# All six rank steps of the 2-of-4 choice on the vector engine, none on GpSimd

## The chip, the core and the metric

One core of a Trainium2 chip runs the whole program as one launch. Its engines run their own instruction streams and meet only at semaphores: TensorE (PE in the profile), VectorE (DVE), ScalarE (ACT), GpSimd (POOL) and SyncE (SP), which issues the DMAs. The metric is the device time of one execution in microseconds, as the median of several runs.

## What is computed

The input is 2 sequences of 2048 tokens of width 256. Four layers follow one another, each with a residual and a layer normalisation: an attention over channels, an MLP with 4-bit weights, a state-space layer, and a gated MLP that keeps 2 of every 4 hidden values. The change touches the last one alone:

```python
def _sparsify_2to4(h):
    g = h.reshape(B, S, I // 4, 4)
    a = jnp.abs(g)
    _, idx = jax.lax.top_k(a, 2)
    pos = jnp.arange(4)
    mask = (pos == idx[..., 0:1]) | (pos == idx[..., 1:2])
    return (g * mask.astype(g.dtype)).reshape(B, S, I)
h = jax.nn.silu(jnp.einsum('bsh,hi->bsi', x, w_gate)) * jnp.einsum('bsh,hi->bsi', x, w_up)
h_sparse = _sparsify_2to4(h)
return jnp.einsum('bsi,ih->bsh', h_sparse, w_down)
```

The hidden width I is 1024. The result goes through one more residual and layer normalisation.

## The kernel before

The first three layers take the time up to about 1067 us of the profiled span and are not touched. The last stage works on 8 groups of 512 tokens. The hidden values of a group are two units of 4 x 128 channels, so there are 16 units, m = 0 to 15; unit m belongs to group m // 2. Within a unit the index r = 0 to 3 is the place of a channel in its foursome, so the four values that compete lie in four tiles `dh[:, mb, r]` of 128 x 512 at the same address of each. Matmuls run at fp32 accuracy as three passes over a high and a low part (`exact3`, lines 44 to 46), so every operand of a matmul needs its low part, which is the value less its rounded copy.

The engines do for each unit, in a static order:

- TensorE, per r: the gate and the up projection (`gate_and_up`, 12 matmuls of 512 columns), then the down projection of the unit two before (`down1`, 12 matmuls of 256 columns), which needs `dhh` and `dhl`. In the second unit of a group, at r = 1, eight transposes of the next group's input stand between (L1616). The first projection of a group waits for the group's low parts `xt_l`, which VectorE makes in `x3_lo` at the end of the unit before. The projection r + 2 waits for `gated1` of r (semaphore `d_mul`).
- ScalarE, per r: silu of the gate (L916), the absolute value of `dh` (L951) and, in r = 2 and 3, the rounded copies `dhh` of the unit before (`kept_hi`, a copy recorded at L670), two in each r. It also makes the high parts of the next input and keeps the residual.
- VectorE, per r: one part of the choice for the unit before (`sparsify`), then `gated1` of this unit (L1279). Part 0 compares value 0 with values 1 to 3, part 1 compares 1 with 2 and 3 and 2 with 3 (L1297: the six `beats` tiles, bf16 zeros and ones). Part 2 forms the ranks (`add_ranks`) and keeps r = 0 and 1 (`keep`, L1313), part 3 keeps r = 2 and 3. In the first unit of a group the output of the group two before is finished between these: `add_x3` (L1337) ahead of part 0, `out_stats` (L1036) ahead of part 1, `normalise` (L1346) ahead of part 3. The last unit of a group ends with `x3_lo` (L1023) for the next one.
- GpSimd, per unit: `ranks`, two steps each for ranks 2 and 3 (L641, L642, L644, L646), then the four subtractions that give `dhl` (L653). The first unit of a group is preceded by `inv_std` (L520, L522) for the output being finished.

A rank is a sum of the comparisons that concern one value. VectorE sums ranks 0 and 1 in three instructions (L1302 of 1024 columns, L1304 and L1305 of 512), GpSimd sums ranks 2 and 3 in four of 512 columns, at the same time, from the same `beats`. The keeps of r = 0 and 1 wait for `d_add` (VectorE), those of r = 2 and 3 for `d_padd` (GpSimd). GpSimd's order puts the ranks of a unit ahead of its subtractions. Groups 2 to 6 run in a loop over the groups; after the last projections the tail on VectorE is `add_x3`, the whole choice for unit 15, then the output of groups 6 and 7, where group 7 waits for the store of group 6 (one output buffer `rows_out`).

Of the kernel before, what the change touches and what calls it, by code (L numbers as in the profile page):

```python
# [5 lines left out]
ALU = mybir.AluOpType  # L6
# [27 lines left out]
RANK = 4  # L34
MB = MLP1 // RANK // P
DT_STEPS = 11
FIX = 5
RES = 4
W1_PIECE = 3 * KT * MLP1 // GROUPS
# [9 lines left out]
def build(nc, x_in, xt_in, codes, scales, w_in, conv_w, conv_b, dt_bias, a_log, d_skip, norm_w, w_out, w_mlp1, out):  # L49
    ctx = ExitStack()  # L50
    with ctx:
# [3 lines left out]
        def sem(name):  # L55
            return ctx.enter_context(nc.semaphore(name))
# [161 lines left out]
        def ds(name, shape, dt=F32):  # L218
            return sb(name, shape, dt, phase_d)
# [6 lines left out]
        beats = ds("beats", [P, 6, TOK], BF16)  # L226
        rank = ds("rank", [P, RANK, TOK], BF16)
# [112 lines left out]
        d_mul = sem("mlp1_gated_ready")  # L340
        d_abs = sem("mlp1_abs_ready")
        d_cmp = sem("pairs_compared")
        d_add = sem("ranks_dve")
        d_padd = sem("ranks_pool")
        d_sel = sem("kept_ready")
        d_hi = sem("kept_hi_ready")
        d_lo = sem("kept_lo_ready")
# [16 lines left out]
        PAIRS = [(0, 0, 3), (1, 3, 2), (2, 5, 1)]  # L364
# [129 lines left out]
        def _(pool):  # L494
# [53 lines left out]
            def halo_terms(n, b):  # L548
# [5 lines left out]
                pool.tensor_tensor(hpart[:, 1, :, 0:1], tail[:, b, :, 2:3], weight[2], ALU.mult).then_inc(c_fix, 1)  # L554
                pool.wait_ge(c_fix, FIX * n + 2)
                pool.tensor_tensor(hfix[:, b, :, 0:2], hfix[:, b, :, 0:2], hpart[:, 0, :, 0:2], ALU.add).then_inc(c_fix, 1)
                pool.wait_ge(c_fix, FIX * n + 4)
                pool.tensor_tensor(hfix[:, b, :, 0:1], hfix[:, b, :, 0:1], hpart[:, 1, :, 0:1], ALU.add).then_inc(c_fix, 1)
# [7 lines left out]
            def masked_decay(n, t):  # L566

                if t == 0:
                    pool.wait_ge(c_dtc, DT_STEPS * (n + 1))
                    pool.wait_ge(c_seg, NT * n)  # L570
# [65 lines left out]

            pool.wait_ge(c_x3, NT * GROUPS)

            def ranks(m):
                pool.wait_ge(d_cmp, len(PAIRS) * (m + 1))  # L640
                pool.tensor_tensor(rank[:, 2], beats[:, 5], beats[:, 1], ALU.subtract).then_inc(d_padd, 1)  # L641
                pool.tensor_tensor(rank[:, 3], beats[:, 2], beats[:, 4], ALU.add).then_inc(d_padd, 1)  # L642
                pool.wait_ge(d_padd, 4 * m + 1)
                pool.tensor_tensor(rank[:, 2], rank[:, 2], beats[:, 3], ALU.subtract).then_inc(d_padd, 1)  # L644
                pool.wait_ge(d_padd, 4 * m + 2)
                pool.tensor_tensor(rank[:, 3], rank[:, 3], beats[:, 5], ALU.add).then_inc(d_padd, 1)  # L646

            def unit(m, mb):

                ranks(m)  # L650
                for r in range(RANK):
                    pool.wait_ge(d_hi, RANK * m + r + 1)
                    pool.tensor_tensor(dhl[:, mb, r], dab[:, mb, r], dhh[:, mb, r].bitcast(F32),  # L653
                                       ALU.subtract).then_inc(d_lo, 1)

            for m in range(3):
                unit(m, m % MB)
            with pool.Fori(2, GROUPS) as g:
                inv_std(g - 2, mv, ve, rstd, d_ln, d_lnr)
                unit(MB * g - 1, 1)  # L660
                unit(MB * g, 0)
# [6 lines left out]
        def _(act):  # L668
            def copy(dst, src):
                return act.activation(dst, src, ACT.Copy)  # L670
# [96 lines left out]
            def xbc_in(n, b, j, place=None, in_xc=False):  # L767

                src = place if place is not None else XBC_LANE[j]
                act.wait_ge(c_xbc, XB * n + j + 1)  # L770
                if place is None:
                    act.wait_ge(c_silu, XB * n + max(j - 1, 0))
                act.wait_ge(c_fix, FIX * (n + 1))
                copy(tail[:, b, j], src[:, TOK - TAPS + 1:])
                act.activation(xc[:, b, j] if in_xc else acc[:, j % 2], src[:], ACT.Identity, bias=cb[:, j:j + 1],
                               scale=cw[:, j, TAPS - 1:TAPS]).then_inc(c_xin, 1)
# [16 lines left out]
            def dt_exp_ln(n, b, mid=True):  # L793
                act.wait_ge(c_dtc, DT_STEPS * n + 2)
                act.activation(de[:], dax[:], ACT.Exp).then_inc(c_dta, 1)
                if mid:
                    xbc_in(n, b, 0)
                act.wait_ge(c_dtc, DT_STEPS * n + 3)
                act.activation(dl[:], du[:], ACT.Ln).then_inc(c_dta, 1)
# [176 lines left out]
        def _(dve):  # L976
# [167 lines left out]
            def conv(n, b, j, in_xc=False, in_early=False):  # L1144
                sums = xc[:, b, j] if in_xc else acc[:, j % 2]
                src = early(j) if in_early else XBC_LANE[j]
                dve.wait_ge(c_xin, XB * n + j + 1)
                dve.wait_ge(c_fix, FIX * (n + 1))
                dve.tensor_tensor(sums[:, 0:TAPS - 1], sums[:, 0:TAPS - 1], hfix[:, b, j], ALU.add).then_inc(c_cv, 1)  # L1149
# [6 lines left out]
            def dt_chain(n, b, mid=True):  # L1156


                def done(k, ins):
                    ins.then_inc(c_dtc, 1)  # L1160
                    dve.wait_ge(c_dtc, DT_STEPS * n + k)

# [137 lines left out]
            def add_ranks(m):  # L1300
                dve.wait_ge(d_cmp, len(PAIRS) * (m + 1))
                dve.tensor_tensor(rank[:, 0:2], beats[:, 1:4:2], beats[:, 2:5:2], ALU.add).then_inc(d_add, 1)  # L1302
                dve.wait_ge(d_add, 3 * m + 1)
                dve.tensor_tensor(rank[:, 0], rank[:, 0], beats[:, 0], ALU.add).then_inc(d_add, 1)  # L1304
                dve.tensor_tensor(rank[:, 1], rank[:, 1], beats[:, 0], ALU.subtract).then_inc(d_add, 1)  # L1305

            def keep(m, mb, r):
                if r < 2:
                    dve.wait_ge(d_add, 3 * m + 2 + r)
                else:  # L1310
                    dve.wait_ge(d_padd, 4 * m + 1 + r)
                value, op = KEEP[r]
                dve.scalar_tensor_tensor(dab[:, mb, r], rank[:, r], value, dh[:, mb, r], op, ALU.mult).then_inc(d_sel, 1)  # L1313

            def sparsify(m, mb, part):
                if part == 0:
                    compare(m, mb, 0)
                if part == 1:
                    compare(m, mb, 1)
                    compare(m, mb, 2)  # L1320
                if part == 2:
                    add_ranks(m)
                    keep(m, mb, 0)
                    keep(m, mb, 1)
                if part == 3:
                    keep(m, mb, 2)
                    keep(m, mb, 3)
# [56 lines left out]
        def _(pe):  # L1384
# [156 lines left out]
            def segment_sums(n, t):  # L1541
                if t == 0:
                    pe.wait_ge(c_zs, NT * n + 1)
                    pe.wait_ge(c_dtc, DT_STEPS * (n + 1))
                elif t == 1:
# [9 lines left out]
            def in_proj_at(n, j):  # L1555
                if j == 2:
                    pe.wait_ge(c_dtc, DT_STEPS * n + 1)
                if j > 2:
# [252 lines left out]
```

## Time and profile before

| | us |
|---|---|
| median of 3 runs | 1367.37 (1366.83 to 1368.35) |
| the profiled execution | 1377.32 |
| its span | 1375.6 |
| busy in the span: PE, DVE, ACT, POOL | 1281.5, 912.1, 608.8, 464.7 |
| last stage, about 1067 to 1375.6 | 308.6 |
| busy there, DVE L1313 (keeps), x64 | 80.2 |
| busy there, POOL L653 (low parts), x64 | 100.3 |
| busy there, POOL rank steps, x64 | 88.5 |

The shares over the whole span mix four layers with different limits, so only rows of the last stage bear on the change. In a row of the timeline the columns are the start, the duration, the engine and the line, the tiles written and read, and in brackets the idle time of the engine before it with what ended that. Two VectorE instructions can overlap by some 0.08 us in these records, so the cost of one in a full queue is the difference of two starts. Several instructions merged in one row have a count behind the x.

### The profile page before, as it was taken

To read this page: it belongs to the slowest core of one execution; us is meant where nothing else is said; L and a number is where in the kernel's file an instruction comes from. 1 tells how busy PE (TensorE), PEld (TensorE's weight loads), DVE (VectorE), ACT (ScalarE), POOL (GpSimd) and SP (SyncE) were. 2 spreads that over 40 slices of the span, in tenths; PEclk is the share of its full clock that TensorE was granted. 3 is DMA by queue.
4 is the path that set the end of the run, shared out by engine and by line. 5 is a ranking of instruction groups with operands and counts; after the bars stand their busy time and mean duration, and the time that the engine had idled before them with its cause. 6 is when DMAs were issued, how large, how long until landed. Compare 5 with 4: busy or idle time off the path is not lost.

```text
span 1375.6 us, 20883 instructions
## 1 busy us (share of the span) xinstructions
PE 1281.5 (93%) x7224; PEld 1068.2 (78%) x7224; DVE 912.1 (66%) x1734; ACT 608.8 (44%) x1125; POOL 464.7 (34%) x568
## 2 busy tenths in 40 slices
PE   6699999999999999999899999999999799999994
PEld 6577888888888888888667767767767687888884
DVE  3486645453534444446588678678676799999997
ACT  3243323232323232334666666666664444444441
POOL 1244300000000000000354554453444566677775
PEclk9899999999999999999899999999999999999997
DMA  4122101000000001000000110010110101010000
GB/s 179 51 77 96 31 1 31 1 16 16 1 31 0 30 0 46 0 16 1 28 26 18 35 43 9 33 43 8 35 43 16 39 1 31 30 30 30 30 16 31
DMA packets 30404, 41.38 MB, mean 30 GB/s; under 512 B 2433, under 2 KB 22913, under 8 KB 30209
## 3 DMA queue, kind: packets, MB, share of 16 engines
q1 hardware_dynamic: 30336, 40.53, 9.0%
q8 instruction: 36, 0.59, 0.2%
q14 instruction: 32, 0.25, 0.1%
HBM read 27.94 MB, written 12.58 MB: 29 GB/s over the span
## 4 chain that ended last, share of the span: by engine, by line
PE 61%; DVE 22%; issue 9%; ACT 6%; POOL 1%; DVEq 1%; DMA 1%; ACTq 0%; POOLq 0%; SPq 0%; PEldq 0%
PE bank L44 18%; PE bank L46 17%; PE bank L45 17%; DVE acc L1153 3%; DVE dab L1313 2%; DVE beats L1297 2%; PE bank L1666 2%; PE bank L1672 2%; DVE dh L1279 2%; DVE rows_out L1346 1%; DVE mag L984 1%; DVE rank L1302 1%; PE bank L1655 1%; DVE st L1036 1%; PE bank L1634 1%
## 5 line engine op out<-in xcount | busy, mean ns | idle before, releaser
L1060 DVE TENSOR_TENSOR hb<-gl,bank 128x512 f32<-128x512 f32 x128 | 87.9, 687 | 200.1 <-PE bank L46 197.5
L670 ACT ACTIVATE hh<-hb 128x512 fp32r<-128x512 f32 x128 | 80.9, 632 | 182.2 <-DVE hb L1060 182.2
L709 ACT ACTIVATE gl<-bank 128x512 f32<-128x512 f32 x128 | 76.4, 597 | 181.8 <-PE bank L46 181.7
L1023 DVE TENSOR_TENSOR hl<-hb,hh 128x512 fp32r<-128x512 f32 x128 | 95.6, 747 | 84.5 <-ACT hh L670 84.5
L520 POOL TENSOR_TENSOR veb<-mvb,eps 128x4 f32<-128x4 f32 x8 | 1.8, 228 | 378.7 <-DVE mvb L1040 378.7
L44 PE MATMUL bank<-xt_l,w_h 128*128 128x512 f32 x256 | 103.8, 406 | 17.9 <-DVE xt_l L1023 15.6
L653 POOL TENSOR_TENSOR dhl<-dab,dhh 128x512 fp32r<-128x512 f32 x64 | 100.3, 1590 | 31.1 <-ACT dhh L670 31.1
L44 PE MATMUL bank<-at_l,w_hi_a 128*128 128x512 f32 x256 | 102.9, 402 | 1.3 <-DVE at_l L1023 1.0
L46 PE MATMUL bank<-xt_h,w_h 128*128 128x512 f32 x256 | 101.9, 398 | 0.0
L46 PE MATMUL bank<-at_h,w_hi_a 128*128 128x512 f32 x256 | 101.8, 398 | 0.0
L45 PE MATMUL bank<-xt_h,w_l 128*128 128x512 f32 x256 | 101.8, 398 | 0.0
L46 PE MATMUL bank<-at_h,w_hi_b 128*128 128x512 f32 x256 | 101.6, 397 | 0.0
L45 PE MATMUL bank<-at_h,w_lo_a 128*128 128x512 f32 x256 | 101.3, 396 | 0.0
L44 PE MATMUL bank<-at_l,w_hi_b 128*128 128x512 f32 x256 | 101.0, 394 | 0.0
L45 PE MATMUL bank<-at_h,w_lo_b 128*128 128x512 f32 x256 | 100.8, 394 | 0.0
L1153 DVE SCALAR_TENSOR_TENSOR acc<-bank,cw,acc 128x509 f32<-128x509 f32 (+2 forms) x108 | 80.9, 749 | 4.0 <-DVE acc L1149 0.2
L44 PE MATMUL bank<-w_l,dhh 128*128 128x256 f32 x256 | 75.0, 293 | 7.0 <-POOL dhl L653 3.8
L1313 DVE SCALAR_TENSOR_TENSOR dab<-rank,dh 128x512 f32<-128x512 bf16 x64 | 80.2, 1293 | 0.0
L44 PE MATMUL bank<-w_lo_a,hh 128*128 128x256 f32 x256 | 73.0, 285 | 4.9 <-DVE hl L1023 4.9
L44 PE MATMUL bank<-w_lo_b,hh 128*128 128x256 f32 x256 | 73.0, 285 | 3.5 <-DVE hl L1023 3.5
L45 PE MATMUL bank<-w_h,dhl 128*128 128x256 f32 x256 | 74.1, 290 | 0.0
L46 PE MATMUL bank<-w_h,dhh 128*128 128x256 f32 x256 | 74.1, 289 | 0.0
(222 smaller groups left out, 3781.2 us busy)
## 6 DMA issues: line engine op xcount, KB each, us to landing
xg<-x_scratch SPq DMA_DIRECT2D x16, 512.0 KB, 3.9
xall<-in_x SPq DMA_DIRECT2D x8, 512.0 KB, 7.3
xg<-in_xt SPq DMA_DIRECT2D x8, 512.0 KB, 4.8
x_scratch<-rows_out SPq DMA_DIRECT2D x8, 512.0 KB, 3.2
x_scratch<-rows_out SPq DMA_DIRECT2D x16, 256.0 KB, 2.2
out<-rows_out SPq DMA_DIRECT2D x8, 512.0 KB, 3.2
wq<-in_codes SPq DMA_DIRECT2D x12, 256.0 KB, 2.6
sc<-in_scales SPq DMA_DIRECT2D x12, 256.0 KB, 2.9
```

Source lines behind the costliest of these rows:

```text
L44: pe.matmul(out, w_hi, m_lo, start=start, stop=False, **kw)
L45: pe.matmul(out, w_lo, m_hi, start=False, stop=False, **kw)
L46: return pe.matmul(out, w_hi, m_hi, start=False, stop=stop, **kw)
L653: pool.tensor_tensor(dhl[:, mb, r], dab[:, mb, r], dhh[:, mb, r].bitcast(F32), ALU.subtract).then_inc(d_lo, 1)
L670: return act.activation(dst, src, ACT.Copy)
L709: act.activation(gl[:, n % 2], ps_gate[n % 2][:], ACT.Gelu_apprx_tanh).then_inc(s_gelu, 1)
L1023: return dve.tensor_tensor(dst, src, hi.bitcast(F32), ALU.subtract)
L1060: dve.tensor_tensor(hb[:, n % 2], gl[:, n % 2], ps_up[n % 2][:], ALU.mult).then_inc(s_h, 1)
L1153: dve.scalar_tensor_tensor(sums[:, late:], src[:, 0:TOK - late], cw[:, j, tap:tap + 1], sums[:, late:], ALU.mult, ALU.add).then_inc(c_cv, 1)
L1279: dve.tensor_tensor(dh[:, mb, r], dg[:, r % 2], up[:], ALU.mult).then_inc(d_mul, 1)
L1297: dve.tensor_tensor(beats[:, to:to + count], dab[:, mb, one:one + 1].broadcast_to([P, count, TOK]), dab[:, mb, one + 1:], ALU.is_ge).then_ ...
L1313: dve.scalar_tensor_tensor(dab[:, mb, r], rank[:, r], value, dh[:, mb, r], op, ALU.mult).then_inc(d_sel, 1)
```

## The change

GpSimd's `ranks` is removed together with its semaphore `d_padd`; GpSimd keeps `inv_std` and the four subtractions of each unit. `add_ranks` on VectorE grows from three instructions to six: a second one of 1024 columns forms the first sums of ranks 2 and 3 together, and two of 512 columns finish them. All four keeps wait for `d_add`, which now counts six steps for each unit. Comparisons, keeps, types and buffers stay, and so does the place of every other instruction.

```diff
+RANK_STEPS = 6
-        d_add = sem("ranks_dve")
-        d_padd = sem("ranks_pool")
+        d_add = sem("rank_steps")
-            def ranks(m):
-                pool.wait_ge(d_cmp, len(PAIRS) * (m + 1))
-                pool.tensor_tensor(rank[:, 2], beats[:, 5], beats[:, 1], ALU.subtract).then_inc(d_padd, 1)
-                pool.tensor_tensor(rank[:, 3], beats[:, 2], beats[:, 4], ALU.add).then_inc(d_padd, 1)
-                pool.wait_ge(d_padd, 4 * m + 1)
-                pool.tensor_tensor(rank[:, 2], rank[:, 2], beats[:, 3], ALU.subtract).then_inc(d_padd, 1)
-                pool.wait_ge(d_padd, 4 * m + 2)
-                pool.tensor_tensor(rank[:, 3], rank[:, 3], beats[:, 5], ALU.add).then_inc(d_padd, 1)
-                ranks(m)
                 dve.tensor_tensor(rank[:, 0:2], beats[:, 1:4:2], beats[:, 2:5:2], ALU.add).then_inc(d_add, 1)
-                dve.wait_ge(d_add, 3 * m + 1)
+                dve.tensor_tensor(rank[:, 2:4], beats[:, 1:3], beats[:, 3:5], ALU.add).then_inc(d_add, 1)
+                dve.wait_ge(d_add, RANK_STEPS * m + 1)
                 dve.tensor_tensor(rank[:, 0], rank[:, 0], beats[:, 0], ALU.add).then_inc(d_add, 1)
                 dve.tensor_tensor(rank[:, 1], rank[:, 1], beats[:, 0], ALU.subtract).then_inc(d_add, 1)
+                dve.wait_ge(d_add, RANK_STEPS * m + 2)
+                dve.tensor_tensor(rank[:, 2], beats[:, 5], rank[:, 2], ALU.subtract).then_inc(d_add, 1)
+                dve.tensor_tensor(rank[:, 3], beats[:, 5], rank[:, 3], ALU.add).then_inc(d_add, 1)
             def keep(m, mb, r):
-                if r < 2:
-                    dve.wait_ge(d_add, 3 * m + 2 + r)
-                else:
-                    dve.wait_ge(d_padd, 4 * m + 1 + r)
+                dve.wait_ge(d_add, RANK_STEPS * m + 3 + r)
```

## Rows read from the trace of the kernel before

**Rows 1.** The page, part 1: busy time and share of the span.

```profile
PE 1281.5 (93%) x7224; PEld 1068.2 (78%) x7224; DVE 912.1 (66%) x1734; ACT 608.8 (44%) x1125; POOL 464.7 (34%) x568
```

**Rows 2.** Window: length; busy PE, PEld, DVE, ACT, POOL; granted clock; DMA share; GB/s.

```profile
1199.10:1235.70 36.60, 34.92 (x202) 30.38 (x201) 35.60 (x47) 16.23 (x28) 26.01 (x18) 1.00 0.09 29
```

**Rows 3.** Waits of the last stage: who, total us, times, longest.

```profile
PE bank L44 <- DVE xt_l L1023: 15.6, 6, 6.5
...
DVE dh L1279 <- PE bank L46: 7.1, 5, 1.9
DVE beats L1297 <- ACT dab L951: 5.3, 7, 0.8
```

**Rows 4.** Timeline of PE: first projection of groups 1 to 5 and 7.

```profile
1085.57 0.76 PE L44 MATMUL bank<-xt_l,w_h 128*128 128x512 f32 x1 [6.55 <-DVE xt_l L1023]
...
1121.56 0.28 PE L46 MATMUL bank<-w_h,dhh 128*128 128x256 f32 x1
1121.86 0.50 PE L44 MATMUL bank<-xt_l,w_h 128*128 128x512 f32 x1
...
1159.37 0.50 PE L44 MATMUL bank<-xt_l,w_h 128*128 128x512 f32 x1 [2.43 <-DVE xt_l L1023]
...
1197.31 0.50 PE L44 MATMUL bank<-xt_l,w_h 128*128 128x512 f32 x1 [1.45 <-DVE xt_l L1023]
...
1233.93 0.50 PE L44 MATMUL bank<-xt_l,w_h 128*128 128x512 f32 x1 [1.68 <-DVE xt_l L1023]
...
1307.27 0.47 PE L44 MATMUL bank<-xt_l,w_h 128*128 128x512 f32 x1 [1.77 <-DVE xt_l L1023]
```

**Rows 5.** Timeline of DVE: ranks and keeps of one group's two units.

```profile
1205.52 0.68 DVE L1302 TENSOR_TENSOR rank<-beats 128x1024 bf16<-128x1024 bf16 x1
...
1208.73 3.23 DVE L1313 SCALAR_TENSOR_TENSOR dab<-rank,dh 128x512 f32<-128x512 bf16 x2
1211.89 0.68 DVE L1279 TENSOR_TENSOR dh<-dg,bank 128x512 f32<-128x512 f32 x1
...
1222.92 1.28 DVE L1302 TENSOR_TENSOR rank<-beats 128x1024 bf16<-128x1024 bf16 x1
...
1226.74 2.25 DVE L1313 SCALAR_TENSOR_TENSOR dab<-rank,dh 128x512 f32<-128x512 bf16 x2
1228.91 0.67 DVE L1279 TENSOR_TENSOR dh<-dg,bank 128x512 f32<-128x512 f32 x1
```

**Rows 6.** Timeline of POOL in the same unit: first rank step, first low parts.

```profile
1205.86 1.37 POOL L641 TENSOR_TENSOR rank<-beats 128x512 bf16<-128x512 bf16 x1
...
1211.37 3.06 POOL L653 TENSOR_TENSOR dhl<-dab,dhh 128x512 fp32r<-128x512 f32 x2
```

**Rows 7.** Timeline of DVE, then POOL, while POOL's ranks had already ended.

```profile
1097.76 0.41 DVE L1305 TENSOR_TENSOR rank<-rank,beats 128x512 bf16<-128x512 bf16 x1
1098.09 1.28 DVE L1313 SCALAR_TENSOR_TENSOR dab<-rank,dh 128x512 f32<-128x512 bf16 x2
1099.30 0.67 DVE L1279 TENSOR_TENSOR dh<-dg,bank 128x512 f32<-128x512 f32 x1
...
1099.52 5.96 POOL L653 TENSOR_TENSOR dhl<-dab,dhh 128x512 fp32r<-128x512 f32 x4 [1.96 <-ACT dhh L670]
```

**Rows 8.** Timeline of DVE at the start: ranks of unit 0 to `gated1`.

```profile
1074.48 1.34 DVE L1302 TENSOR_TENSOR rank<-beats 128x1024 bf16<-128x1024 bf16 x1
...
1080.51 0.68 DVE L1279 TENSOR_TENSOR dh<-dg,bank 128x512 f32<-128x512 f32 x1
```

**Rows 9.** Timeline of the tail: PE, DVE twice, POOL.

```profile
1341.04 0.28 PE L46 MATMUL bank<-w_h,dhh 128*128 128x256 f32 x1
...
1342.98 1.41 DVE L1337 TENSOR_TENSOR rows_out<-bank,res 128x256 f32<-128x256 f32 x4
...
1348.21 0.69 DVE L1302 TENSOR_TENSOR rank<-beats 128x1024 bf16<-128x1024 bf16 x1
...
1354.03 6.33 POOL L653 TENSOR_TENSOR dhl<-dab,dhh 128x512 fp32r<-128x512 f32 x4
```

## The prediction, made before the changed kernel was run

> **What bounds the kernel now.** The page's busy shares come first, and they mislead: TensorE leads with 93% and VectorE has 66% [rows 1]. The change lies only in the last stage, so I cut that stage into groups. One group of the loop takes 36.60 us, of which VectorE is busy 35.60, TensorE 34.92, GpSimd 26.01 and ScalarE 16.23, at full granted clock [rows 2]. Two engines are close. The waits decide between them: TensorE waits 15.6 us for `xt_l`, which VectorE makes last in a group, in six waits, one at each handover but one [rows 3]. The other way VectorE waits for TensorE only 7.1 us in five waits, nearly all of it in group 1, and 0.7 to 0.8 us for ScalarE at the start of a group's second unit [rows 3]. So VectorE is the bound from group 2 on, and TensorE the next one, 1.7 us behind in each group.
>
> How far behind is read from the handovers. From 1197.31 to 1233.93 a group takes 36.62, and 1.68 of it is TensorE idle ahead of the second start [rows 4]. The handover at 1121.86 shows what is left when VectorE is ahead: the last matmul ended at 1121.56 + 0.28 = 1121.84, so 0.02 is idle [rows 4]. TensorE's own period is therefore 36.62 - 1.68 + 0.02 = 34.96 us.
>
> **What the change removes and adds on VectorE.** VectorE and GpSimd slow each other. A rank step of 512 columns took 0.41 us while GpSimd had nothing to do (it idled 1.96 us up to 1099.52), and the next started 0.33 after it; two keeps then took 1099.30 - 1098.09 = 1.21 [rows 7]. Beside GpSimd's rank steps the same block of three steps takes 1208.73 - 1205.52 = 3.21 us in the first unit of a group and 1226.74 - 1222.92 = 3.82 in the second, and the two keeps behind it 3.16 and 2.17 [rows 5]; GpSimd's four steps start 0.34 after VectorE's first and its low parts at 1211.37 [rows 6], so they cover the whole block and most of the keeps.
>
> The new block, with GpSimd idle: a step of 1024 columns that had a free path took 0.68 [rows 5], 0.60 start to start by the overlap of 0.08; two of these and four of 512 at 0.33 make 1.20 + 1.32 = 2.52 us. The new waits are on VectorE's own semaphore for steps that lie one or more instructions back and cost nothing as long as the free path holds; behind them are the keeps and `gated1`, for which TensorE waits two projections later. I take 2.52; from above the bound is the contended price, 2 x 1.28 + 4 x 1.20 = 7.4. Is GpSimd idle then? Its previous work is the low parts of the unit before, and it can start the next low part only after keep 0 and ScalarE's copy, in the slack row 1.96 us after its last rank step [rows 7]. In the first unit of a group `inv_std` can touch the first step; its price is at most one step, 0.7.
>
> Keeps 0 and 1 then run free as well: 1.21, since ScalarE needs about 0.7 from keep 0 to its copy and only then GpSimd returns. Sum for a group: ranks (3.21 - 2.52) + (3.82 - 2.52) = 1.99, keeps (3.16 - 1.21) + (2.17 - 1.21) = 2.91, together 4.90. VectorE needs 36.62 - 4.90 = 31.7 us. That is 3.2 under TensorE's 34.96, so the bound changes side and only 36.62 - 34.96 = 1.66 of the 4.90 is cashed in a steady group. The 3.2 covers what I leave at nothing: the touch of `inv_std` (0.7), and keeps 2 and 3 and `normalise` colliding with low parts as they do now.
>
> A rule speaks for dearer collisions. Two keeps beside GpSimd took 3.23, or 1.6 each [rows 5]. The Trainium skill, page "SBUF — State Buffer", section "SBUF: two separate sides", says that the shared port pair is held for a whole instruction and that the loser fully blocks. In strict turns a keep (0.60) and a GpSimd step (1.37) would take 2.0; as an estimate by that rule the eight low parts of a group add 8 x 0.4 = 3.2 us, VectorE needs 34.9, and nothing is left of the slack, though the forecast would stand. The trace shows 1.6, so it disagrees on the size.
>
> **GpSimd** loses 4 steps of 1.2 to 1.6 us in a unit and keeps the low parts; it was not on the path inside the loop. Its freed time costs nothing. No DMA moves, no queue of SP is passed, ScalarE's order stays.
>
> **The sum over the stage.**
> Start: from the ranks of unit 0 to `gated1` VectorE needs 1080.51 - 1074.48 = 6.03 [rows 8]; after, 2.52 + 1.21 = 3.73. TensorE idles 6.55 behind it [rows 4], so 2.3 us is gained in full. Group 1 up to 1121.86 is already TensorE's: nothing.
> Groups 2 to 6: 1307.27 - 1121.86 = 185.41 [rows 4] becomes 5 x 34.96 = 174.8, a gain of 10.6. It is more than 5 x 1.66 because two of these groups took 37.5 and 37.9: the first ends in 2.43 idle, and the second begins with slower matmuls behind that idle (37.94 less its own 1.45 of idle is 36.5, 1.5 above TensorE's period), which go with the wait.
> Group 7: `add_x3` starts at 1342.98, though the down projection that it needs ended at 1341.04 + 0.28 = 1341.32 [rows 9]. VectorE is now the late one; afterwards it would be ready long before, so the gain is 1.6.
> Tail: GpSimd ends its rank steps before it may start the low parts, at 1354.03, 5.8 after VectorE's compares end at 1348.21, and ends at 1354.03 + 6.33 = 1360.36 [rows 9]. After: ranks 2.52, keep 0 0.68, ScalarE 0.7, so low parts start at +3.9; keeps 2 and 3 still collide, and four low parts at about 1.4 end at +9.5 instead of +12.15. Gain 2.5 (1.9 if the low parts stay at 6.33). What follows, `inv_std`, two outputs and their stores, keeps its length.
> Total 2.3 + 10.6 + 1.6 + 2.5 = 17.0 us. The profiled execution took 1377.3 and would take 1360.3. Its time is 10 us above the median of the runs; I carry the difference and not the ratio (1% of 17 is nothing): 1367.4 - 17.0 = 1350.4.
>
> **Rivals.**
> A, the collisions come back elsewhere and VectorE stays the bound. Condition: over 3.2 of the 4.9 us return in each group, through low parts that hit the rank block or the keeps. For it: GpSimd now starts its low parts 5 us earlier, while VectorE is still in keeps or `normalise`, and 3.23 for two keeps shows the price [rows 5]. Against: the number of low parts is the same, and each can delay one instruction only; they collide already now. If the group takes 36.0, 5 groups give 5 x (37.08 - 36.0) = 5.4, and with start, tail and group 7 at half, 3, the time is about 1359.
> B, slower: the rank steps are dear on VectorE whether GpSimd is idle or not, 1.28 and 1.20. Against it stand the 0.41 and the 0.68 [rows 5, 7]; for it only that nearly all other rows show the high price. Two blocks of 7.4 replace 7.03 and the keeps give back 2.9: the group takes 36.62 + 14.8 - 7.03 - 2.9 = 41.5. Five groups +22, group 7 +5, start and tail +4: about 1398. It decides from the point where the twelve steps of a group average (4.9 + 5.04) / 12 = 0.83 us; below that the group cannot be slower than now.
> C, no effect: the unprofiled runs are bound by TensorE throughout, and only start and tail remain. The handover row with 0.02 idle shows that such a group exists [rows 4], but the profile has it only where VectorE had no output to finish. It would still give about 1363; no change at all needs A and C together.
>
> **How the numbers follow.** Forecast 0.72: 1350.4, own range 1346 to 1355 (low end: the slower matmuls behind the start's idle, a first one of 0.76 for 0.50 [rows 4], go too, 36.29 - 34.96 = 1.3 us of group 1, and 3 us for the timed runs differing from the profiled one; high end: 0.7 us more at each handover, tail gain 1.9). A 0.16, 1355 to 1363. B 0.06. C and smaller gains 0.06, of which 0.03 within 0.2%. I take 1345 to 1361, which leaves out B, C and the upper edge of A. A measurement can tell 0.2%, 2.7 us, from no change. Faster by more: 0.72 + 0.16 + 0.03 = 0.91; within 0.03; slower 0.06.
>
> **What would show it.** Right: rank steps of 512 columns at 0.41 us and of 1024 at 0.68, keeps 0 and 1 at about 1.2 for two; VectorE waiting for TensorE at `gated1` several times in each group; TensorE's wait for `xt_l` near 0 after group 1 and 4.3 instead of 6.55 ahead of it; group starts 35.0 apart; the low parts of unit 15 ending some 9.5 after the last compare. Wrong: rank steps at 1.2 or more (B), or VectorE without a wait for TensorE and groups near 36 (A).

## The result, and the profile after the change

The changed kernel takes 1355.47 us, the median of its runs (1353.26 to 1360.03), where the kernel before, run beside it, takes 1367.86 (1366.83 to 1373.23). The ratio is 0.9884, with an interval of 0.9858 to 0.9910: faster by 1.2%. The forecast was 1350.4 with a range of 1345 to 1361. The profiled execution took 1360.03 us, of which 1358.3 is its span; the one before took 1377.3 and 1375.6.

The span's difference of 17.3 us is not all the change's. In all traces of this study the work ahead of the last stage is the same code, yet the stage begins between 1059.9 and 1069.9 us. So from here on I measure the last stage alone: from the start of the first comparison of unit 0 on VectorE to the end of the span. Before, it takes 305.73 us, and 305.77 in a second profile of the same kernel. After, it takes 290.13, and 289.99 in a second profile. The change is worth 15.6 us of stage; (1367.4 - 15.6) / 1367.4 = 0.9886, inside the interval.

The page, part 1, of the changed kernel (busy us and share for each engine; it answers to [rows 1]):

```profile
PE 1278.9 (94%) x7224; PEld 1066.1 (78%) x7224; DVE 879.8 (65%) x1782; ACT 607.9 (45%) x1125; POOL 374.5 (28%) x504
```

VectorE carries 48 instructions more and is busy 32 us less. One group's window (length; busy PE, PEld, DVE, ACT, POOL; granted clock; DMA share; GB/s), which answers to [rows 2]:

```profile
1189.00:1224.00 35.00, 34.93 (x201) 30.41 (x200) 31.86 (x54) 16.07 (x28) 14.72 (x10) 1.00 0.10 30
```

TensorE fills the group, 34.93 of 35.00. VectorE needs 31.86 for 54 instructions, where it needed 35.60 for 47. The waits of the last stage (who waited for whom: total us, times, longest), for [rows 3]:

```profile
DVE dh L1268 <- PE bank L47: 21.0, 24, 2.9
...
PE bank L45 <- DVE xt_l L1012: 4.5, 2, 4.3
```

The two have changed places: VectorE waits for TensorE in 24 places, and TensorE's wait for `xt_l` has gone from 15.6 us in six places to 4.5 in two: 4.33 ahead of group 1 and 0.16 ahead of group 7. The timeline of PE at the start of group 1 and at a handover inside the loop (start, duration, operation, in brackets the idle time before it and what ended it), for [rows 4]:

```profile
1081.65 0.76 PE L45 MATMUL bank<-xt_l,w_h 128*128 128x512 f32 x1 [4.33 <-DVE xt_l L1012]
...
1188.75 0.28 PE L47 MATMUL bank<-w_h,dhh 128*128 128x256 f32 x1
1189.10 0.50 PE L45 MATMUL bank<-xt_l,w_h 128*128 128x512 f32 x1
```

At the handover into a group the last matmul ends at 1188.75 + 0.28 = 1189.03 and the next starts at 1189.10, so 0.07 us are left. The timeline of DVE in the first unit of the same group, for [rows 5]:

```profile
1198.25 0.68 DVE L1291 TENSOR_TENSOR rank<-beats 128x1024 bf16<-128x1024 bf16 x1
...
1199.46 0.41 DVE L1294 TENSOR_TENSOR rank<-rank,beats 128x512 bf16<-128x512 bf16 x1
...
1200.80 1.28 DVE L1303 SCALAR_TENSOR_TENSOR dab<-rank,dh 128x512 f32<-128x512 bf16 x2
1202.00 0.68 DVE L1268 TENSOR_TENSOR dh<-dg,bank 128x512 f32<-128x512 f32 x1
```

Six rank steps take 1200.80 - 1198.25 = 2.55 us, less than three took before (3.21), and the two keeps behind them 1.20 instead of 3.16. Over all sixteen units no step of 512 columns took more than 0.42 and none of 1024 more than 0.70.

The stage cut into its terms, by the start of `xt_l` on VectorE, which is the same marker in both kernels:

| term | before | after | gain | forecast |
|---|---|---|---|---|
| first comparison to `xt_l` of group 1 | 14.87 | 12.65 | 2.2 | 2.3 |
| group 1 | 36.38 | 37.50 | -1.1 | 0 |
| groups 2 to 6 together | 185.33 | 175.08 | 10.25 | 10.6 |
| group 7: `xt_l` to `add_x3` | 36.53 | 34.94 | 1.6 | 1.6 |
| from there to the end | 32.6 | 30.0 | 2.7 | 2.5 |
| sum | 305.7 | 290.1 | 15.6 | 17.0 |

### The profile page after: what moved, and what is told of

It reads as the page before. It is cut to its first block, busy times and chain, and to the rows that moved or that the text cites. A ratio compares the mean times of both kernels' runs of the same rounds, so it can differ in the third digit from the quotient of the medians.

```text
span 1358.3 us, 20875 instructions
## 1 busy us (share of the span) xinstructions
PE 1278.9 (94%) x7224; PEld 1066.1 (78%) x7224; DVE 879.8 (65%) x1782; ACT 607.9 (45%) x1125; POOL 374.5 (28%) x504
## 4 chain that ended last, share of the span: by engine, by line
PE 76%; DVE 13%; ACT 6%; issue 3%; POOL 1%; DMA 0%; DVEq 0%; ACTq 0%; POOLq 0%; SPq 0%; PEldq 0%
PE bank L45 23%; PE bank L47 22%; PE bank L46 22%; DVE acc L1142 3%; PE bank L1656 2%; PE bank L1662 2%; DVE mag L973 1%; PE bank L1645 1%; PE bank L1624 1%; ACT L800 1%; PE bank L1498 1%; DVE wf L981 1%; ACT yo L852 1%; DVE state L1241 1%; ACT hh L659 1%
## 5 line engine op out<-in xcount | busy, mean ns | idle before, releaser
L642 POOL TENSOR_TENSOR dhl<-dab,dhh 128x512 fp32r<-128x512 f32 x64 | 96.4, 1528 | 141.5 <-ACT dhh L659 141.5
L1286 DVE TENSOR_TENSOR beats<-dab 128x1536 bf16<-128x1536 f32 (+2 forms) x48 | 66.5, 1414 | 9.5 <-ACT dab L940 5.3
```

The source lines that it names most:

```text
L1286: dve.tensor_tensor(beats[:, to:to + count], dab[:, mb, one:one + 1].broadcast_to([P, count, TOK]), dab[:, mb, one + 1:], ALU.is_ge).then_ ...
```

## The experiments

My theory: GpSimd's rank steps and its low parts hold up VectorE, a removed collision is worth far more than the added steps cost, and inside the loop TensorE's 35.0 us caps the gain. The rivals: it is the waits on GpSimd's semaphore or the order that went, not the collisions; VectorE's margin behind TensorE is as thin as before; the low parts that GpSimd keeps still cost something. All stage lengths in one table; a group is the mean of groups 2 to 6, and the ratio is of timed runs against the kernel before on the same chip.

| kernel | stage us | group us | ratio (interval) |
|---|---|---|---|
| before | 305.73 | 37.07 | 1 |
| before again (e9) | 305.77 | 37.06 | |
| after | 290.13 | 35.02 | 0.9884 (0.9858 to 0.9910) |
| after again (e1) | 289.99 | 35.02 | 0.9873 (0.9848 to 0.9898) |
| e2, GpSimd busy with spare steps | 333.42 | 40.71 | 1.0181 (1.0156 to 1.0206) |
| e3, before with a shorter down projection | 310.27 | 37.92 | 1.0043 (1.0023 to 1.0062) |
| e4, after with a shorter down projection | 271.35 | 32.46 | 0.9767 (0.9746 to 0.9788) |
| e5, two ranks only | 286.63 | 35.0 | 0.9859 (0.9824 to 0.9893) |
| e6, low parts on VectorE too | 287.14 | 35.0 | 0.9855 (0.9818 to 0.9892) |
| e11, the same again | 288.62 | 35.0 | 0.9869 (0.9842 to 0.9896) |
| e7, tail split between two engines | 290.98 | 35.0 | 0.9891 (0.9851 to 0.9930) |
| e8, everything on VectorE, tail reordered | 288.42 | 35.0 | 0.9869 (0.9840 to 0.9897) |
| e10, half of the move | 293.04 | 35.18 | 0.9908 (0.9877 to 0.9940) |

### e1_change_again: the change repeated

> The changed kernel once more, timed in more rounds. The median of its first runs lay 12.4 us under before, while the last stage is 15.6 us shorter in its trace. If the trace is what a timed run does, the difference is 14 to 17 us (time near 1352); if something outside the stage takes a part back, it stays near 12 (1355).

Measured: 1356.25 against 1373.42, 17.2 us, and a stage of 289.99. The same kernel before has medians of 1367.86 and 1373.42 on the two occasions, and the gains read from medians are 12.4 and 17.2; the stage gives 15.6 and 15.8 in the profiled executions. So the difference between the occasions most likely lies outside the stage; the timed runs have no trace that would show it.

### e2_gpsimd_steps_kept: the collisions put back alone

```
             def unit(m, mb):
+                pool.wait_ge(d_cmp, len(PAIRS) * (m + 1))
+                pool.wait_ge(d_spare, 4 * m + 1)
+                pool.tensor_tensor(spare[:, 2], spare[:, 0], spare[:, 1], ALU.subtract).then_inc(d_spare, 1)
+                pool.tensor_tensor(spare[:, 3], spare[:, 1], spare[:, 0], ALU.add).then_inc(d_spare, 1)
...
```

> The changed kernel, and GpSimd keeps four steps of 512 columns at the place of its old rank steps, on a tile of its own that nobody else reads or writes; output unchanged. Collision theory: four of VectorE's six rank steps cost 1.2 to 1.28 us again, the block about 5.6 and block plus first two keeps 6.8 instead of 3.7; a group takes about 37.9 us, and the time is 1366 to 1380, no better than before. Rival (the gain came from the keeps and low parts no longer waiting for GpSimd's ranks, not from collisions): rank steps stay at 0.41 and 0.68, the time stays at 1355.

Measured: 1399.47, a stage of 333.42, 43.3 us above the changed kernel, whose VectorE list it has word for word. Nobody reads what GpSimd computes here. The timeline of DVE, then of POOL, in one unit of it:

```profile
1214.08 0.69 DVE L1303 TENSOR_TENSOR rank<-beats 128x1024 bf16<-128x1024 bf16 x1
1214.68 1.66 DVE L1304 TENSOR_TENSOR rank<-beats 128x1024 bf16<-128x1024 bf16 x1
1216.26 1.39 DVE L1306 TENSOR_TENSOR rank<-rank,beats 128x512 bf16<-128x512 bf16 x1
1217.57 1.38 DVE L1307 TENSOR_TENSOR rank<-rank,beats 128x512 bf16<-128x512 bf16 x1
...
1220.17 0.41 DVE L1310 TENSOR_TENSOR rank<-beats,rank 128x512 bf16<-128x512 bf16 x1
```

```profile
1214.31 1.48 POOL L646 TENSOR_TENSOR spare<-spare 128x512 bf16<-128x512 bf16 x1
1215.75 1.62 POOL L647 TENSOR_TENSOR spare<-spare 128x512 bf16<-128x512 bf16 x1
1217.33 1.34 POOL L649 TENSOR_TENSOR spare<-spare 128x512 bf16<-128x512 bf16 x1
1218.63 1.34 POOL L651 TENSOR_TENSOR spare<-spare 128x512 bf16<-128x512 bf16 x1
```

Four GpSimd steps hold four VectorE steps, one each; the first and the last of the block, outside them, cost 0.60 and 0.34 from start to start. So the gain hung on GpSimd being silent, not on the waits or the order, and the rival of a changed wait falls. The direction was as expected and the size was not: the block took 6.43 us (6.14 in the group's other unit) for the expected 5.6, since the step of 1024 columns beside GpSimd takes 1216.26 - 1214.68 = 1.58, and the group 40.8 for 37.9. Of these 2.9 the two blocks of a group give 6.43 + 6.14 - 2 x 5.6 = 1.4. Another 0.9 to 1.2 is VectorE waiting for TensorE, which idles 3.5 to 3.8 us ahead of groups 3 to 6 (7.8 ahead of group 1) and comes back with slow matmuls, as in e3 below.

### e3_before_two_pass_down and e4_after_two_pass_down: less work for TensorE

```
-                    mm = exact3(pe, down_tile[t], dhh[...], dhl[...], w1h[...], w1l[...], ...)
+                    pe.matmul(down_tile[t], dhl[:, mb, r, t * P:(t + 1) * P], w1h[:, at:at + H], start=first, ...)
+                    mm = pe.matmul(down_tile[t], dhh[:, mb, r, t * P:(t + 1) * P], w1h[:, at:at + H], ..., stop=last, ...)
```

The same edit to the kernel before (e3) and to the changed one (e4): the product of the down projection with the low part of its weights is left out, so TensorE has about 3.8 us less to do in a group, and nothing else is touched.

> The kernel before, and the down projection of the last stage leaves out the pass over the weights' low part (part of the computation left out): 16 matmuls of 256 columns less in each unit, 1.9 us of TensorE, 3.8 in each group. If VectorE bounds the groups 2 to 6 as read, they keep 36.6 us and only group 1 and the tail gain, 4 to 7 us in all (time 1360 to 1364). If TensorE were the bound, the gain would be near 30 us (1338).

> The changed kernel with the same pass left out. If TensorE is the bound after the change and VectorE needs 31.7 us in a group, TensorE's 31.2 falls under it: groups of 32 to 32.5, VectorE hardly waiting for TensorE, time about 20 us under the changed kernel (1335). If collisions make VectorE's own need larger than was read (34 us), groups end at 34 and the time at 1346 or above.

Measured, e4 first: 1341.92, a stage of 271.35. Windows of its groups 2 to 4:

```profile
1115.90:1148.90 33.00, 31.61 (x171) 26.52 (x169) 32.06 (x54) 16.74 (x30) 14.73 (x10) 1.00 0.11 33
1148.90:1180.90 32.00, 31.12 (x168) 26.56 (x168) 31.07 (x53) 15.42 (x28) 14.70 (x10) 1.00 0.10 33
1180.90:1213.50 32.60, 31.10 (x168) 26.56 (x168) 31.66 (x53) 16.37 (x30) 14.73 (x10) 1.00 0.10 32
```

With its cover gone VectorE keeps a pace of 32.0 to 33.0, busy 31.1 to 32.1 of it, and in groups 2 to 6 it never waits for TensorE. The mean of 32.46 is VectorE's own period, 0.8 more than the forecast's 31.7; its margin behind TensorE was 35.0 - 32.5 = 2.5 us and not 3.2, but it was there. The time was expected 20 us under the changed kernel (1335). It is 14.3 under that kernel's 1356.25 on the same occasion (e1), while the stage is 18.6 shorter; in the two traces the stage begins at 1069.15 here and at 1062.21 in e1, so the rest lies in the untouched part ahead of it.

e3 fell outside its expectation. VectorE being the bound, its group should have stayed at 36.6 and the time with it; the stage grew by 4.5 us to 310.27, and the timed runs by 0.4%. A window of a group, then the timeline of PE at the handover and of DVE behind it:

```profile
1189.50:1227.30 37.80, 33.19 (x168) 27.76 (x168) 35.61 (x47) 15.96 (x28) 26.11 (x19) 0.95 0.09 28
```

```profile
1228.08 0.50 PE L44 MATMUL bank<-xt_l,w_h 128*128 128x512 f32 x1 [3.72 <-DVE xt_l L1023]
...
1228.94 0.63 PE L44 MATMUL bank<-xt_l,w_h 128*128 128x512 f32 x1
1229.36 0.63 PE L45 MATMUL bank<-xt_h,w_l 128*128 128x512 f32 x1
```

```profile
1232.80 0.69 DVE L1279 TENSOR_TENSOR dh<-dg,bank 128x512 f32<-128x512 f32 x1 [1.18 <-PE bank L46]
```

VectorE's busy time is the same as before, 35.61 [rows 2], which is the part that was expected. New is that TensorE, now idle for 3.7 us at each handover, comes back slow: matmuls of 0.63 that start 0.43 apart where they start 0.24 apart otherwise, a granted clock of 0.95 in the window, the 1.2 GHz level for the length of them. VectorE, at that moment short of nothing but the first projection, waits 1.18 for it. A non-bounding engine was given slack, and the bounding one paid.

### e5_two_ranks_only: how much the added steps cost

```
-                ranks(m)
...
-                dve.scalar_tensor_tensor(dab[:, mb, r], rank[:, r], value, dh[:, mb, r], op, ALU.mult).then_inc(d_sel, 1)
+                dve.scalar_tensor_tensor(dab[:, mb, r], rank[:, r % 2], value, dh[:, mb, r], op, ALU.mult).then_inc(d_sel, 1)
```

Made from the kernel before: ranks 2 and 3 are formed by nobody, and their keeps read ranks 0 and 1.

> The kernel before without GpSimd's rank steps and without anything in their place: the keeps of r = 2 and 3 use ranks 0 and 1 (ranks 2 and 3 are left out). VectorE then has 1.4 us of rank steps in a unit. If the new steps on VectorE are free inside the groups because TensorE bounds them, the groups stay at 35.0 us as in the changed kernel and only start and tail gain 1.2 us each: 288 us from the first comparison to the end against 290.1. If the three added steps cost anything in the loop, the groups get shorter than 35.0.

Measured: a stage of 286.63, groups of 35.0. A kernel without those steps at all is 3.5 us of stage ahead of the changed one, about 1.1 at the start, 1.0 in group 1 and 1.3 in the tail, and level with it in groups 2 to 6. The 1.0 in group 1 is not the price of the steps: seven slow matmuls stand there instead of twelve (last section). The steps that VectorE took over are free where TensorE covers them.

### e10_gpsimd_one_rank: half of the move

```
-                pool.tensor_tensor(rank[:, 2], beats[:, 5], beats[:, 1], ALU.subtract).then_inc(d_padd, 1)
...
+                dve.tensor_tensor(rank[:, 2], beats[:, 5], beats[:, 1], ALU.subtract).then_inc(d_add, 1)
...
+                dve.tensor_tensor(rank[:, 2], rank[:, 2], beats[:, 3], ALU.subtract).then_inc(d_add, 1)
```

GpSimd keeps rank 3, two steps a unit; VectorE has five.

> Half of the change: rank 2 moves to VectorE (two steps of 512 columns), rank 3 stays on GpSimd (two steps). Collision theory: each GpSimd step still holds up one VectorE step by about 0.95 us, so the block takes about 3.9 to 4.5 us instead of 2.52, the first two keeps are free (1.21), VectorE needs 34.5 to 35.7 in a group: at TensorE's 35.0, groups of 35.0 to 36.0, 292 to 297 us from the first comparison to the end (290.1 with the whole change, 305.7 before). If instead the gain came all at once with the last use of GpSimd, the groups would stay near 36.6.

Measured: a stage of 293.04, groups of 35.05 and 35.27 in turn, as expected. The timeline of DVE and of POOL in one unit, and a window of a group:

```profile
1233.35 1.38 DVE L1300 TENSOR_TENSOR rank<-beats 128x512 bf16<-128x512 bf16 x1
1234.66 1.38 DVE L1302 TENSOR_TENSOR rank<-rank,beats 128x512 bf16<-128x512 bf16 x1
1235.96 0.41 DVE L1303 TENSOR_TENSOR rank<-rank,beats 128x512 bf16<-128x512 bf16 x1
```

```profile
1233.09 1.37 POOL L641 TENSOR_TENSOR rank<-beats 128x512 bf16<-128x512 bf16 x1
1234.53 1.22 POOL L643 TENSOR_TENSOR rank<-rank,beats 128x512 bf16<-128x512 bf16 x1
```

```profile
1189.00:1224.00 35.00, 34.68 (x201) 30.18 (x200) 34.07 (x51) 15.98 (x28) 19.94 (x15) 1.00 0.10 30
```

Two GpSimd steps, two dear VectorE steps: 1.30 from start to start instead of 0.33. The block takes 3.88 us in this unit and 3.51 in the group's other one, at and below the lower end of the expected 3.9 to 4.5. VectorE's busy time in a group falls with the number of GpSimd's rank steps in a unit: 35.6 for four [rows 2], 34.1 for two, 31.9 for none. Already the first half brings the group down to 35.18 on average, and the second half brings only 0.16 more, because TensorE is met.

### e6_low_parts_on_vectore and e11_low_parts_again: GpSimd left with almost nothing

```
-            def unit(m, mb):
-                for r in range(RANK):
-                    pool.wait_ge(d_hi, RANK * m + r + 1)
-                    pool.tensor_tensor(dhl[:, mb, r], dab[:, mb, r], dhh[:, mb, r].bitcast(F32),
...
+            def low(m, mb, r):
+                dve.wait_ge(d_hi, RANK * m + r + 1)
+                lo_part(dhl[:, mb, r], dab[:, mb, r], dhh[:, mb, r]).then_inc(d_lo, 1)
```

The low parts go to VectorE as well, one in each r of the unit two later.

> The changed kernel, and VectorE also makes the low parts of the kept values (four of 512 columns in each unit, one unit later, one in each r); GpSimd keeps inv_std alone. Collision theory: every rank step, keep and compare runs at its free price, VectorE needs about 32.5 us in a group although it has 4.8 more to do, the groups stay at 35.0 (TensorE), the wait of TensorE at the start shrinks by 1.9, the tail grows by about 1: 289 us from the first comparison to the end. Rival (the number of VectorE's instructions counts, not their collisions): VectorE needs 31.7 + 4.8 = 36.5 and the groups take 36.5, 300 us.

> The kernel with the low parts on VectorE too, in more rounds: its last stage took 287.1 us in the trace, 3.0 under the changed kernel, 1.1 longer in the tail and 4.1 shorter at the start and in group 1. If that repeats, the stage takes 287 to 288.5 and the timed runs lie 16 to 20 us under before; the spread of the runs of some us may hide the 3 us against the changed kernel.

Measured: groups of 35.0 in both, stages of 287.14 (289 expected) and 288.62 (just above the expected 287 to 288.5). The groups of instructions on DVE in one group of the loop (count | busy us, mean ns | idle before), of e6 and then the same operations in the changed kernel:

```profile
L1001 DVE TENSOR_TENSOR dhl<-dab,dhh 128x512 fp32r<-128x512 f32 x8 | 5.5, 682 | 0.0
L1292 DVE SCALAR_TENSOR_TENSOR dab<-rank,dh 128x512 f32<-128x512 bf16 x8 | 5.1, 681 | 0.0
...
L1325 DVE TENSOR_SCALAR rows_out<-rows_out,mv,rstd 128x256 f32<-128x256 f32 x4 | 1.4, 404 | 0.0
```

```profile
L1303 DVE SCALAR_TENSOR_TENSOR dab<-rank,dh 128x512 f32<-128x512 bf16 x8 | 6.5, 854 | 0.0
...
L1336 DVE TENSOR_SCALAR rows_out<-rows_out,mv,rstd 128x256 f32<-128x256 f32 x4 | 3.0, 814 | 0.0
```

Eight low parts add 5.5 us of busy time, and keeps and `normalise` (and the comparisons) give nearly all of it back: VectorE is busy 32.28 in a group for 61 instructions, against 31.86 for 54. What slows VectorE is the company, not the count. It gains nothing inside the loop, where TensorE already sets the pace. At the start it gains 1.7 to 1.8 us; group 7 and the tail together lose 1.1: `add_x3` of group 6 starts 1.6 later, behind four low parts that now queue ahead of it on VectorE, and what follows is 0.5 shorter. The 1.5 us between the two runs of this one program come from where TensorE's slow stretch falls (last section). The timed runs don't separate it from the change.

### e7_tail_split and e8_all_on_vectore_tail: the tail

```
-            unit(MB * GROUPS - 1, 1)
-            for g in (GROUPS - 2, GROUPS - 1):
-                inv_std(g, mv, ve, rstd, d_ln, d_lnr)
+            inv_std(GROUPS - 2, mv, ve, rstd, d_ln, d_lnr)
+            unit(MB * GROUPS - 1, 1, 2)
+            inv_std(GROUPS - 1, mv, ve, rstd, d_ln, d_lnr)
...
+            for r in (2, 3):
+                dve.wait_ge(d_hi, RANK * (MB * GROUPS - 1) + r + 1)
+                lo_part(dhl[:, 1, r], dab[:, 1, r], dhh[:, 1, r]).then_inc(d_lo2, 1)
```

This is e7: two of the last four low parts go to VectorE, and group 6's output moves ahead of them. e8 is e6 with the same thought, the output of group 6 placed between the low parts of the last two units.

> The changed kernel with another tail: statistics of group 6 ahead of unit 15's choice, and low parts 2 and 3 of unit 15 on VectorE after group 6's normalisation, 0 and 1 on GpSimd. The groups are untouched; group 7's output starts 2.3 us earlier: 287.8 us from the first comparison to the end. If the tail is bound by something else (the store of group 6, the down projections), it stays at 290.1.

> All low parts on VectorE and the other order of the tail together: group 6's statistics ahead of unit 15's choice, its normalisation between the last low parts. Collision theory: groups 35.0, start 1.9 shorter, tail 2.0 shorter: 286.2 us from the first comparison to the end, 4 us under the changed kernel. If VectorE becomes the bound with its longer list, the groups exceed 35.0 and the gain is lost.

Measured: e7 has a stage of 290.98 for the 287.8 expected, e8 288.42 for 286.2. Neither shortened the tail. e7, timeline of DVE and then of PE:

```profile
1339.57 3.28 DVE L1337 TENSOR_SCALAR rows_out<-rows_out,mv,rstd 128x256 f32<-128x256 f32 x4
1342.77 1.28 DVE L1013 TENSOR_TENSOR dhl<-dab,dhh 128x512 fp32r<-128x512 f32 x2
1349.08 1.09 DVE L1328 TENSOR_TENSOR rows_out<-bank,res 128x256 f32<-128x256 f32 x3 [5.03 <-PE bank L47]
```

```profile
1340.83 0.58 PE L45 MATMUL bank<-w_l,dhh 128*128 128x256 f32 x1 [5.47 <-POOL dhl L643]
1341.21 0.41 PE L46 MATMUL bank<-w_h,dhl 128*128 128x256 f32 x1
```

The `normalise` that I had moved ahead ran beside GpSimd's low parts and took 3.28 us, where e6 had 1.4 busy for the same four, and this held back VectorE's own low parts. It was not what cost the time, though: TensorE, idle for 5.47 up to GpSimd's first low part, ran its last 48 matmuls without another wait. The first 23 took 0.37 to 0.58 and started 0.21 apart, where they take 0.28 [rows 9] and start 0.12 apart in the loop. The last of the 48 ended at 1349.04, and `add_x3` waited 5.03 for them. In e8 the same, PE and then DVE:

```profile
1331.35 0.58 PE L45 MATMUL bank<-w_l,dhh 128*128 128x256 f32 x1 [6.04 <-DVE dhl L1001]
```

```profile
1338.83 1.41 DVE L1316 TENSOR_TENSOR rows_out<-bank,res 128x256 f32<-128x256 f32 x4 [4.44 <-PE bank L47]
```

So the rival named in the expectation of e7 held: once group 6's store is no longer what `add_x3` waits for (3.04 us in the changed kernel), the last down projection is. My expectations priced it at TensorE's full clock. By the starts of its matmuls against 0.12 apart the slow ones add 2.3 us in e7, where the stage missed by 3.2, and 1.5 in e8, where it missed by 2.2. The changed kernel has 1.6 of such slowness there too, hidden behind the wait for the store. That no arrangement of the tail helps is not shown; these two don't.

### e9_before_again: the ruler

> The kernel before once more, for a second trace. The last stage, from the first comparison of unit 0 to the end of the span, took 305.7 us in the first trace, while the untouched part ahead of it took 1062 to 1070 us in traces of kernels that are the same there. If the stage is fixed by its order of work, it takes 305.7 again (within 0.5) wherever it starts; if the gain of 15.6 is partly chance, it differs by some us.

Measured: a stage of 305.77 (305.73 in the first profile), each term of it within 0.1 us, while the stage began 4.6 us earlier. So differences of 1 us of stage between two kernels can be read, unless TensorE's slow stretch falls elsewhere.

## Why the prediction was right, and where its terms were off

**The bound.** Right: VectorE was the bound from group 2 on and TensorE the next one. TensorE's wait for `xt_l` is near nothing after group 1, and e4 shows that it is TensorE which holds VectorE back now.

**The price of the block and the keeps.** Right: 2.52 forecast and 2.55 measured, 1.21 and 1.20. The touch of `inv_std`, left at nothing with up to 0.7 in reserve, costs nothing: block and keeps of that unit together, 1202.00 - 1198.25 = 3.75, are at the free price.

**VectorE's need in a group.** Mis-sized, by what I left at nothing. The forecast of 31.7 is a period, 36.62 - 4.90, and about 1.0 of it is waits. As busy time it says 35.60 - 4.90 = 30.7, and 31.86 was measured, so 1.2 of the 4.90 came back elsewhere. The period itself is seen in e4, at 32.46. The widest comparison in one group, first of the changed kernel and then of the kernel before (count | busy us, mean ns | idle before):

```profile
L1286 DVE TENSOR_TENSOR beats<-dab 128x1536 bf16<-128x1536 f32 x2 | 4.4, 2178 | 0.8 <-ACT dab L940 0.8
```

```profile
L1297 DVE TENSOR_TENSOR beats<-dab 128x1536 bf16<-128x1536 f32 x2 | 3.5, 1751 | 0.8 <-ACT dab L951 0.8
```

It gives 0.9 of the 1.2 and `normalise` 0.3 (3.0 for 2.7). GpSimd's low parts now run earlier, from 1189.40 to 1191.96 at the start of a group, and the comparison that starts at 1190.97 takes 2.60 instead of 1.74. The margin behind TensorE covered this, so the time doesn't show it.

**Only the first 1.7 of 4.9 cashed.** Right: e10 and e5 show it from both sides. The group came out at 35.02 and not 34.96; five times 0.06 is the 0.3 by which groups 2 to 6 fell short. 0.05 of each 0.06 is the handover: I took the 0.02 idle of 1121.86 for all of them, and inside the loop 0.07 is left (row 1189.10).

**The dearer collisions of the rule.** The estimate that stood beside the forecast, 34.9 us of need, is refuted in size: e4 ran at 32.0 to 33.0 with the eight low parts in it. Part of its excess is my own working. It took the GpSimd step at 1.37, its price in company, which already holds a wait. With the 1.12 that it takes alone, a keep and a step come to 1.72, and 3.16 / 2 = 1.58 was measured (last section).

**Start.** 2.2 for 2.3, right. TensorE's idle time was to fall from 6.55 to 4.3 and fell to 4.33.

**Group 1.** This is the step that failed. I put "nothing" there, and at the low end even a gain of 1.3, on the thought that a shorter idle time leaves fewer slow matmuls. It left more. The end of the slow stretch on PE, before and then after:

```profile
1088.26 0.52 PE L44 MATMUL bank<-xt_l,w_h 128*128 128x512 f32 x1
1088.62 0.40 PE L45 MATMUL bank<-xt_h,w_l 128*128 128x512 f32 x1
```

```profile
1086.48 0.63 PE L47 MATMUL bank<-xt_h,w_h 128*128 128x512 f32 x1
1086.90 0.35 PE L45 MATMUL bank<-w_l,dhh 128*128 128x256 f32 x1
```

Before, seven matmuls from 1085.57 on were slow behind 6.55 us idle; after, twelve from 1081.65 on behind 4.33, each holding up the next by some 0.2 us, and five more times 0.2 is nearly all of the 1.1 us by which group 1 grew (36.38 to 37.50). In e5, e6, e10 and e11 the same group takes 36.44, 35.04, 37.04 and 36.58. The term should have stood as 0 with 1.2 to either side.

**Group 7.** 1.6 for 1.6, right.

**Tail.** 2.7 for 2.5. The timeline of DVE and of POOL there, for [rows 9]:

```profile
1333.19 0.69 DVE L1291 TENSOR_TENSOR rank<-beats 128x1024 bf16<-128x1024 bf16 x1
...
1335.75 2.49 DVE L1303 SCALAR_TENSOR_TENSOR dab<-rank,dh 128x512 f32<-128x512 bf16 x4
```

```profile
1337.17 5.90 POOL L642 TENSOR_TENSOR dhl<-dab,dhh 128x512 fp32r<-128x512 f32 x4 [7.94 <-ACT dhh L659]
```

The low parts start at +3.98 after the end of the compares (forecast 3.9) and end at +9.88 (9.5): their length, 5.90, lies between the 5.6 and the 6.33 that I had. That is 12.15 - 9.88 = 2.3 of the 2.7. The other 0.4 lies ahead of it, in the three comparisons of unit 15, 3.86 us before and 3.48 after: before, they began at 1344.31 beside GpSimd's low parts of unit 14, which ran to 1344.82; after, those had ended.

**The sum and the time.** 15.6 for 17.0; of the 1.4, group 1 is 1.1 and the steady group 0.3, and start and tail cancel. The predicted time lies 5.1 us under the median. 1.4 is the sum's; the other 3.7 are of the size by which the part ahead of the stage wanders, and I can't tell them from it. The range held because of its upper edge, not because of its centre: the forecast's own 1346 to 1355 was missed by 0.5, and 1355.47 lies where A had put the time. That A's mechanism did not happen is read from the stage, not from the time.

**The rivals.** A did not happen in full: it asked for over 3.2 us of returning collisions in a group, and 1.2 returned. B is refuted by every rank step at 0.41 or 0.68; e2 shows that its prices were those of the company. That e2 came to 40.8 us a group and 1399.5 for B's 41.5 and 1398 is partly luck: the blocks took 6.43 and 6.14 and not 7.4, and waits for a slow TensorE, which B did not have, filled some of the gap. C is refuted, since 10.25 of the 15.6 came from groups 2 to 6 and the timed runs agree with the stage.

## What to carry to other kernels

When two engines slow each other, price an operation by its row with the other engine silent, and look for that row at the start of a stage or in a stretch where one of them is still waiting: six steps alone were cheaper here than three in company. Then cash only the distance to the next bound, since half of the move already brought nine tenths of what a steady group could give. And where an edit leaves TensorE idle for some microseconds, the matmuls behind the idle time belong in the sum at their slow price. When a margin is checked afterwards, compare a period with a period and a busy time with a busy time: 31.7 against 31.86 looked like a hit and hid 1.2 us of returned collisions.

## What the runs showed of the hardware

**A collided pair costs little more than the GpSimd step alone.** In the kernel before VectorE idled from 1092.48 to 1094.28, and GpSimd's first two rank steps of that unit ran like this (timeline of POOL):

```profile
1092.57 1.17 POOL L641 TENSOR_TENSOR rank<-beats 128x512 bf16<-128x512 bf16 x1 [5.98 <-DVE beats L1297]
1093.69 1.16 POOL L642 TENSOR_TENSOR rank<-beats 128x512 bf16<-128x512 bf16 x1
```

Alone, a GpSimd step takes 1.12 from start to start and a VectorE step 0.33; in e2 the pair takes 1.30, less than the sum of 1.45. GpSimd loses 0.18 and VectorE nearly a whole microsecond. A VectorE step of 1024 columns (0.60 alone) and a keep (0.60 alone) come to 1.58 in company [e2, and rows 5], less than 1.72. The Trainium skill, page "SBUF — State Buffer", section "SBUF: two separate sides", says that the pair of ports is an exclusive lock for the whole instruction and the other engine fully blocks. The rows agree that one waits for the other; an overlap of some 0.15 us remains in all three pairs that strict turns would not leave. The opening, which lets the engines meet only at semaphores, is too narrow here. And not every instruction is held up: `add_x3`, which reads a PSUM bank, took 1.42 us beside GpSimd's low parts (start 1189.63) and 1.41 in e8 with GpSimd idle.

**TensorE's slow stretch has a length and a place of its own.** At the start of group 1 seven matmuls were slow behind 6.55 us of idle time (before, e3, e9), ten behind 5.29 (e10), twelve behind 4.33 (after, e1, e4, e7), seven behind 3.21 (e5), nine behind 2.50 (e8, e11) and twelve behind 7.77 (e2): the same idle time gave the same count, but the count doesn't grow with the idle time. One and the same program had the stretch once in group 1 (e11) and once in the unit before it (e6), there behind only 2.35 us of idle time, which stands at the same place in the other traces too, without slow matmuls behind it (timeline of PE of e6):

```profile
1068.97 0.49 PE L45 MATMUL bank<-xt_l,w_h 128*128 128x512 f32 x1 [2.35 <-DVE dh L1257]
...
1069.55 0.63 PE L47 MATMUL bank<-xt_h,w_h 128*128 128x512 f32 x1
```

The slow matmuls start 0.43 apart, which is the 1.2 GHz level, and the others 0.24, the 2.4 GHz level. What decides where the stretch begins and how long it lasts stays open.

**Less work can take longer.** e3 left out 3.8 us of TensorE's work in every group and the stage grew by 4.5 us. VectorE's wait of 1.18 us behind the slow matmuls answers to most of the group's growth from 36.62 to 37.87.
